# Flat maxima, norm scales later, a new order, and the weight groups' loads on Pool's queue

## The reference

```python
x = x + xattn(layernorm(x), ctx, ctx, q_norm_w, k_norm_w, w_out)
x = x + ffn(layernorm(x), ...)
# xattn: 16 query heads on 4 key heads, width 32; RMS norms with weights, rotary positions,
#        scores * 1/sqrt(32), causal mask, softmax, times v, then @ w_out.T
# ffn:   y1 = x1 @ w_up + b_up + x1 @ a_up @ b_up_lora ; x2 = relu(y1)
#        y2 = x2 @ w_down + b_down + x2 @ a_down @ b_down_lora
# w_up, w_down: 2048 x 512 and 512 x 2048, (q - 7.5) * scale, one scale for 64 columns, q stored as int32
```

## Time and profile before

| | us |
|---|---|
| median of 3 runs (lowest, highest) | 485.68 (484.91, 486.22) |
| profiled execution, its time | 485.92 |
| its span, first to last instruction | 484.1 |
| TensorE (PE) busy | 442.8 (91%) |
| VectorE (DVE) busy | 352.2 (73%) |
| ScalarE (ACT) busy | 300.2 (62%) |
| Pool busy | 282.2 (58%) |

### The profile page before, as it was taken

How to read it: one execution, slowest core, us unless ns; L and a number is a source line. 1 busy time by engine, 2 the same in 40 slices (tenths; PEclk the granted TensorE clock), 3 DMA queues, 4 the chain that set the end, 5 groups by cost and what they waited for, 6 DMA issues and landing times.

```text
span 484.1 us, 8263 instructions
## 1 busy us (share of the span) xinstructions
PE 442.8 (91%) x2416; PEld 217.4 (45%) x2416; DVE 352.2 (73%) x1078; ACT 300.2 (62%) x927; POOL 282.2 (58%) x304
## 2 busy tenths in 40 slices
PE   0266859999999999999999999999999999999997
PEld 0254535444444444444444444444444444444443
DVE  3999898979879786868686877778777856544341
ACT  1599788877848575758575766667575846522120
POOL 5367677776758584838484747565666745351100
PEclk9996699999999999999999999999999999999999
DMA  5686869779866877988777687887678677474422
GB/s 147 258 261 142 190 208 213 134 146 144 169 130 123 167 118 154 130 174 123 162 134 152 132 168 131 169 126 159 125 144 158 115 151 113 91 122 97 88 56 74
DMA packets 207372, 70.17 MB, mean 145 GB/s; under 512 B 196912, under 2 KB 199728, under 8 KB 206688
## 3 DMA queue, kind: packets, MB, share of 16 engines
q1 hardware_dynamic: 205760, 69.09, 71.6%
q10 hardware_dynamic: 1488, 0.40, 0.4%
q0 software_dynamic: 80, 0.16, 0.1%
HBM read 16.95 MB, written 4.19 MB: 44 GB/s over the span
## 4 chain that ended last, share of the span: by engine, by line
PE 78%; DVE 1%; DMA 1%; SPq 0%; issue 0%
PE ff L936 33%; PE ff L922 32%; PE tb L904 7%; PE sb L876 2%; PE tb L892 2%; DMA x<-hid 1%; SPq L393 0%; PE tb L862 0%; DVE t_sin L1147 0%; DVE pr L1179 0%; DVE y L1229 0%; DVE stats L1160 0%; DVE x L1157 0%; DVE q L1188 0%; DVE wd_lo L1081 0%; DVE q L1096 0%
## 5 line engine op out<-in xcount | busy, mean ns | idle before, releaser
L936 PE MATMUL ff<-wd_hi,x 128*128 128x512 f16 x512 | 152.3, 379 | 0.6 <-DMA x<-hid 0.6
L922 PE MATMUL ff<-wu_hi,xnT 128*128 128x512 f16 x512 | 152.5, 379 | 0.2 <-ACT wu_lo L641 0.2
L679 ACT ACTIVATE pr<-pr,nmax 128x128 f32<-128x128 f32 x256 | 99.1, 389 | 14.6 <-DVE nmax L1179 13.9
L505 POOL TENSOR_TENSOR big<-pr,big 128x512 f16<-128x512 f32 x64 | 80.9, 1271 | 33.6 <-ACT big L710 33.5
L922 PE MATMUL ff<-wu_lo,xnT 128*128 128x512 f16 x256 | 97.0, 379 | 0.0
L936 PE MATMUL ff<-wd_lo,x 128*128 128x512 f16 x256 | 97.0, 379 | 0.0
L496 POOL TENSOR_TENSOR pr<-pr,rinv 128x512 f32<-128x512 f32 x64 | 72.7, 1137 | 35.7 <-DVE rinv L1089 35.7
L744 ACT ACTIVATE hid<-z 128x512 f16<-128x512 f32 x64 | 39.9, 624 | 80.5 <-DVE z L1110 80.5
L1179 DVE CUSTOM_DVE_ANT_0 pr<-sb,tabs,score_scale 128x128 f32<-128x128 f32 x256 | 73.8, 344 | 12.3 <-PE sb L876 11.2
L922 PEld LDWEIGHTS ff<-wu_hi,xnT 128*128 128x128 f16 x512 | 48.0, 98 | 58.9 <-issue 5.9
L1110 DVE SCALAR_TENSOR_TENSOR z<-ff,su,b_row 128x512 f32<-128x512 f32 x64 | 47.6, 744 | 36.0 <-PE ff L922 34.7
(11 more groups left out here) (149 smaller groups left out, 652.2 us busy)
## 6 DMA issues: line engine op xcount, KB each, us to landing
xt<-in_x SPq DMA_DIRECT2D x16, 256.0 KB, 3.1
big<-in_L_ffn_w_up_q SPq DMA_DIRECT2D x4, 1024.0 KB, 5.6
big<-in_L_ffn_w_down_q SPq DMA_DIRECT2D x4, 1024.0 KB, 6.3
out<-y SPq DMA_DIRECT2D x16, 256.0 KB, 2.7
kvt<-in_ctx SPq DMA_DIRECT2D x16, 64.0 KB, 2.9
wd_lo<-in_L_xattn_w_out SPq DMA_DIRECT2D x1, 1024.0 KB, 7.9
pT<-big SPq DMA_TRANSPOSE x64, 3.5
b_row<-in_L_ffn_b_up SPq DMA_DIRECT2D x1, 1024.0 KB, 9.2
```

Source lines behind the costliest of these rows:

```text
L505: pool.tensor_tensor(p3[:, m, :, 1, :], pr[:, m], p3[:, m, :, 0, :], ALU.subtract).then_inc(p_low, 1)
L679: last = act.activation(pr[:, m, g, :], pr[:, m, g, :], ACT.Exp, bias=nmax[:, p, j:j + 1], scale=-1.0, accum_out=rsum[:, p, j:j + 1])
L922: last = pe.matmul(bank[:], a[:, m, :], b[:, m, 512 * g:512 * g + 512], start=(m == 0 and i == 0), stop=(m == KC - 1 and i == 2))
L936: last = pe.matmul(ff[down_bank[n]][:], x2T[:, part, k + h % HG, :], b[:, h, :], start=(h == 0 and i == 0), stop=(h == HC - 1 and i == 2))
```

## The change

The kernel after differs in these parts:

- The maxima of s_up, of the down lora matrix and of the bias are taken of flat copies with long contiguous pieces (in the third stage buffer); s_up and the down lora matrix are loaded again in their own layout, s_up in four parts. The rest of s_up is scaled later (`later_scales`, ahead of the first VectorE tile from 4 on). The identity part of the tables comes in a load of its own.
- `norm_scales` (with the norm powers in it) and the moments of batch 0 stand in the loop, at slots 19 and 20; only the two maxima of the norm weights stay ahead.
- 13 scale steps in place of 17; the lora halves wait for 10 of them and are done apart for up and down.
- All tables of the order are new. VectorE dequantizes 25 tiles in place of 27 (Pool: 10, 16, 19, 22, 23, 27, 30) and writes 28 low halves in place of 25.
- Group 0 is loaded on SP without its waits. Groups 1 to 7 are loaded from Pool's queue, inside Pool's loop, with the same waits, and group 2 also after the maxima.

```diff
-R_MOMENTS = (0, 23, 473, 1390)
+R_MOMENTS = (20, 77, 760, 1674)
...
-DVE_TILES = (0, 1, 2, 3, 4, 5, 6, 7, 8, 9, 10, 12, 13, 14, 15, 16, 17, 18, 19, 20, 22, 23, 24, 25, 27, 28, 30)
+DVE_TILES = (0, 1, 2, 3, 4, 5, 6, 7, 8, 9, 11, 12, 13, 14, 15, 17, 18, 20, 21, 24, 25, 26, 28, 29, 31)
...
-LOAD_AT = (369, 421, 557, 574, 1092, 1168, 1277)
+LOAD_AT = (182, 210, 281, 692, 890, 1237, 1432)
...
+LORA_D_LOAD_AT, NORM_SCALES_AT = 137, 19
...
+        s_up_flat, a_dn_flat = big[:, 4096:4096 + HC * C // QB], big[:, 4224:4224 + HC * R]
+        b_flat = big[0:HC, 4480:4480 + P]
...
-            def load_group(g):
-                if g >= W_RING:
-                    sp.wait_ge(w_turned, 4 * (g - W_RING + 1))
-                src = wuq_v[g] if g < 4 else wdq_v[g - 4]
-                sp.dma_start(stage_i[:, g % W_RING], src).then_inc(wq_in[g % W_RING], 16)
...
             sp.dma_start(s_dn[:], wds.rearrange("(p c) b -> p c b", p=P)).then_inc(scales_in, 16)
+            sp.dma_start(a_dn_flat, wda.rearrange("(p c) r -> p (c r)", p=P)).then_inc(lora_a_in, 16)
+            sp.dma_start(xt[:, 0, :], x[0]).then_inc(x_in[0], 16)
...
-            load_batch(0)
-            sp.wait_ge(lora_a_in, 16 * 3)
-            sp.wait_ge(k_weight_in, 16)
-            sp.wait_ge(q_weight_in, 16)
-            load_group(0)
+            sp.dma_start(s_up[:, 0:4, :].rearrange("p i b -> p (i b)"), wus_v[0]).then_inc(up_scales_in[0], 16)
+            sp.dma_start(stage_i[:, 0], wuq_v[0]).then_inc(w0_in, 16)
+            for g in range(1, 4):
+                sp.dma_start(s_up[:, 4 * g:4 * g + 4, :].rearrange("p i b -> p (i b)"), wus_v[g]).then_inc(up_scales_in[1], 16)
...
+            def load_group(g):
+                if g >= W_RING:
+                    pool.wait_ge(w_turned, 4 * (g - W_RING + 1))
+                if g == 2:
+                    pool.wait_ge(tops_ready, 7)
+                src = wuq_v[g] if g < 4 else wdq_v[g - 4]
+                pool.dma_start(stage_i[:, g % W_RING], src).then_inc(wq_in[g % W_RING], 16)
...
             for s in range(SLOTS):
+                for g in range(1, 8):
+                    if LOAD_AT[g - 1] == s:
+                        load_group(g)
...
+            def later_scales():
+                dve.wait_ge(up_scales_in[1], 16 * 3)
+                dve.tensor_scalar(s_up[:, 4:, :], s_up[:, 4:, :], kap[:, 0:1], None, ALU.mult).then_inc(scales_ready, 1)
+                dve.wait_ge(scales_ready, 3)
...
             find_tops()
-            norm_powers()
             gather_tops()
             input_stats(0)
-            norm_scales()
-            input_moments(0)
-            take_tops()
+            norm_tops()
             find_scales()
             for s in range(1, SLOTS):
+                if s == NORM_SCALES_AT:
+                    norm_scales()
```

More of the change, by code:

```diff
@@ new lines @@
+R_MOMENTS = (20, 77, 760, 1674)
+R_KEYS = (0, 284, 671, 2018)
+R_POW = (130, 280, 886, 2236)
+R_CENTRE = (18, 59, 913, 1980)
+R_SINES = (44, 152, 960, 1733)
+R_COSINES = (181, 209, 1210, 2240)
+R_ROPE = (108, 341, 980, 1738)
+R_KSPLIT = (45, 407, 1176, 2046)
+R_KLOW = (134, 345, 1081, 1794)
+R_KTURN = (247, 545, 854, 1798)
+R_QSPLIT = (94, 463, 1093, 2051)
+R_QLOW = (146, 410, 1067, 1763)
+R_QTURN = (212, 392, 829, 1794)
+R_SCORES = ((281, 643, 1348, 2033), (480, 674, 1397, 2052), (500, 876, 1551, 2129), (591, 1020, 1692, 2159))
@@ L242, in build @@
         tops_taken = sem("tops_taken")
+        up_scales_in, a_dn_in = [sem(f"up_scales_in{i}") for i in range(2)], sem("a_dn_in")
         scale_steps, scales_ready = sem("scale_steps"), sem("scales_ready")
@@ L754, in _ @@
                 second_norm_high(s)
-                if s == LORA_A_AT:
-                    lora_a_high()
+                for down in range(2):
+                    if LORA_A_AT[down] == s:
+                        lora_a_high(down)
                 if LORA_BHIGH_AT == s:
@@ L1016, in gather_tops, with find_scales @@
                 dve.tensor_scalar(diag8[:], ident[0:8, 0:8], top8[:], None, ALU.mult).then_inc(diag8_ready, 1)
-            def take_tops():
+            def find_scales():
+                bound, power, lora, deq = tmp[:, 0:5], tmp[:, 5:10], tmp[:, 10:12], tmp[:, 12:14]
                 dve.wait_ge(tops_spread, 1)
+                link(dve.tensor_scalar(deq, tb[0][:, 0:2], 7.5 / W_TOP, 1e-30 / W_TOP, ALU.mult, ALU.add), wait=False)
+                link(dve.tensor_scalar(lora, tb[0][:, 2:4], float(R) / W_TOP, None, ALU.mult), wait=False)
+                link(dve.tensor_scalar(bound[:, 2:4], tb[0][:, 2:4], 1e-30, 1.0 / A_TOP, ALU.add, ALU.mult), wait=False)
@@ new lines, in find_scales @@
+                dve.wait_ge(scale_steps, 3)
+                for j in range(2):
+                    link(dve.tensor_scalar(bound[:, j:j + 1], lora[:, j:j + 1], tops_all[:, 4 + j:5 + j], deq[:, j:j + 1], ALU.mult, ALU.add), wait=j > 0)
+                link(dve.tensor_scalar(bound[:, 4:5], bound[:, 0:1], float(C) * W_TOP, tops_all[:, 6:7], ALU.mult, ALU.add))
+                link(dve.tensor_scalar(power.bitcast(I32), bound.bitcast(I32), 0x7F800000, None, ALU.bitwise_and))
+                link(dve.reciprocal(kap[:, 0:5], power))
@@ new lines, in find_scales @@
+                for j in range(2):
+                    link(dve.tensor_scalar(kap[:, 6 + j:7 + j], kap[:, j:j + 1], power[:, 2 + j:3 + j], None, ALU.mult), wait=False)
+                assert step[0] == LORA_STEPS
+                dve.wait_ge(up_scales_in[0], 16)
+                dve.tensor_scalar(s_up[:, 0:4, :], s_up[:, 0:4, :], kap[:, 0:1], None, ALU.mult).then_inc(scales_ready, 1)
+                dve.tensor_scalar(s_dn[:], s_dn[:], kap[:, 1:2], None, ALU.mult).then_inc(scales_ready, 1)
+                link(dve.tensor_scalar(kap[:, 5:6], kap[:, 4:5], X2_TOP, None, ALU.mult))
@@ L1248, in _ @@
                     wout_arg()
-                if s == LORA_ALOW_AT:
-                    lora_a_low()
+                for down in range(2):
+                    if LORA_ALOW_AT[down] == s:
+                        lora_a_low(down)
                 if LORA_BLOW_AT == s:
```

252 lines of the change are left out of this document (117 added, 135 removed).

## The result

The changed kernel takes 495.38 us (median of 4 runs, 493.71 to 497.4), against 485.74 us for the kernel before beside it (484.91 to 486.22): ratio 1.020, 95% interval 1.017 to 1.023. It is slower, as forecast, but by 9.6 us and not by 4.1, and so above the range, which ended at 494.5.

A forecast was written before the change was run, and what follows sets the result against it. VectorE was taken to bound the front, setting when TensorE becomes full. Start 4.0 us earlier, list +6.4, waits +0.8 and Pool's chain put tile 20 5.0 later; minus 0.45 and 0.5 gave +4.1: 489.8 us, range 482.8 to 494.5.

The forecast's parts named there:

- The sign and where it is decided: Whole kernel: slower by 4.1 us, decided before TensorE becomes full at tile 20; the part from 110 us on unchanged.
- The start: Scales ahead of VectorE's loop: last maximum at 8.8 us, then 6.3 us, so the loop begins at 15.0, 4.0 us earlier.
- VectorE's list ahead of tile 19, +6.4 us: VectorE's added work before tile 17's low half frees tile 19's bank, including norm scales, moments and low halves: +6.4 us.
- I take 0.8 us of waits for both: VectorE's waits for the second and third weight groups, loaded from Pool: 0.8 us together, between 0 and 2.5.
- Pool's chain behind tile 19: After tile 19 is turned, Pool issues the last load, then does two dequantizations: 5.2 us before tile 20, starting 5.0 later.
- On SP the moved loads leave room: SP's queue: its 13.6 us of waits at the moved loads go, but a query transpose there was ready no sooner.
- so I count no gain: SP's queue, freed of the moved loads, was given no gain in the sum: 0 us.
- the wait of group 8: Pool's last load, called group 7 in the prediction, waits for tile 19's turn and holds up two dequantizations that tile 20 needs.
- The clock: TensorE at tile 20: a gap over 5 us may drop it to 1.2 GHz, giving 492 us; counted inside the forecast's range.
- The 0.95 us that I took off behind tile 20: TensorE behind tile 20: 0.45 us for two score groups done earlier and 0.5 us of shrinking waits, subtracted.
- Pool's loads are slow: Pool's seven loads cost 1.5 us each to issue or land 2 us late: 493 to 495 us, chance 0.1.

The follow-up runs named there:

- experiment 1: Changed kernel with weight groups 2 to 8 loaded from SP's queue again, order tables as changed: 485.26 us, ratio 0.999.
- experiment 10: Changed kernel, loads on Pool, with the last group's load moved behind the dequantizations of tiles 22 and 23: 491.46 us, ratio 1.013.
- experiment 12: Changed kernel, loads on Pool, with loads of groups 4, 6 and 8 moved behind other work and groups 5 and 7 moved off transpositions: 489.61 us, ratio 1.008.
- experiment 3: Kernel before with groups 2 to 8 loaded from Pool's queue, the first three of these loads placed early: 497.39 us, ratio 1.023.
- experiment 5: Kernel before, loads on SP, with group 8's load one slot earlier, ahead of batch 2's key transposition: 487.90 us, ratio 1.004.
- experiment 4: Kernel before, loads on Pool, first three early, groups 6 and 8 behind the transpositions, SP's three waits for turned tiles kept: 487.58 us, ratio 1.005.
- experiment 6: Kernel before, loads on SP, with group 5's load moved behind batch 1's query and key transpositions: 488.62 us, ratio 1.005.
- experiment 13: Changed kernel, loads on Pool, with the value sums of batch 0 behind tile 8 in TensorE's list: 495.81 us, ratio 1.019.
- experiment 14: Changed kernel with its loads on SP and the value sums of batch 0 behind tile 8 in TensorE's list: 485.36 us, ratio 0.999.
- experiment 7: Kernel before with the new maxima, norm scales and scale steps, old order, loads on SP, group 5's load behind batch 1's transpositions: 488.06 us, ratio 1.004.
- experiment 8: Changed kernel with its loads on SP and group 5's load moved behind batch 1's key transposition: 486.50 us, ratio 1.001.
- experiment 9: Changed kernel, loads on SP, group 5's load behind batch 1's key transposition, value sums of batch 0 behind tile 8: 485.54 us, ratio 1.000.
- experiment 2: Kernel before with only groups 2 to 8 loaded from Pool's queue, every other order as before: 498.25 us, ratio 1.027.

## Why the prediction was wrong

- **The sign and where it is decided: right.** From 120 to 480 us TensorE is busy for 360.0 of 360 us in both kernels; the loss is made ahead of that.
- **The start: too cautious.** The loop begins 5.4 us sooner, not 4.0: the last maximum ends 1.8 us ahead of the 8.8 that I took, and from it to the loop are 6.7 us, not 6.3. The norm scales cost 1.2 us in the loop, not 2.1: two integer instructions of half the size took 0.2 us together and not the 1.19 of the one in the earlier trace rows.
- **VectorE's list ahead of tile 19, +6.4 us: the number right, in part by luck.** With the loads on SP tile 19 is turned at 71.9 (experiment 1); the forecast said 71.7. But the loop begins at 14.1 there and the norm scales are 0.9 us cheaper, so about 1.8 us should have come on top and did not. VectorE, taken as always busy, is idle for 6.2 us from 20 to 100, and what TensorE waits for just ahead of tile 19 is batch 2's scores (1.4 us), not a low half.
- **"I take 0.8 us of waits for both" for groups 2 and 3: right** (0.7 us at VectorE).
- **Pool's chain behind tile 19: right.** From tile 19 turned to tile 20's transposes 4.9 us, forecast 5.2; taken away it gives 3.9 us back (experiment 10).
- **The step that failed is the one on what the moved loads leave behind: "On SP the moved loads leave room", and "so I count no gain".** It asked whether SP would gain and not whether anything would lose by the loads' new place, and it counted them on Pool as issue time and waits alone: its sum has no term for them between group 3 and group 8. The 3.9 us by which tile 19 is later than with the loads on SP are missing there. Between these two traces, which run the same list, the lag grows in three steps. First, Pool's load of group 5 leaves at 43.30, and batch 1's key transposition, at 44.20, lands in 6.3 us; with the loads on SP it lands in 2.5 us (the changed kernel, then experiment 1):

```profile
DMA to landing us min/median/max: 6.3/6.3/6.3
```

```profile
DMA to landing us min/median/max: 2.5/2.5/2.5
```

  The scores of batch 1 wait 3.4 us behind it. But they wait 2.6 us in experiment 1 as well, where group 5's load on SP delays the query transposition instead, and the lag at this place is 1.4 us. Second, Pool stands 4.2 us at the load of group 6, and its work behind that load then runs at the same time as three instructions of VectorE, which take 3.8 us together instead of 2.1. The longest of them, the changed kernel, then experiment 1:

```profile
59.19 1.75 DVE L1099 SCALAR_TENSOR_TENSOR big<-big,s_dn 128x512 f32<-128x512 int32 x1
```

```profile
57.47 0.69 DVE L1099 SCALAR_TENSOR_TENSOR big<-big,s_dn 128x512 f32<-128x512 int32 x1
```

  In experiment 12, where Pool's work lies elsewhere, each of the three takes 0.68 us. With that the first output projection starts 2.9 us late. Third, TensorE has by then waited 3.1 us for it and not 1.7, and does these matmuls at half clock and not at full, 5.1 us in place of 2.6 (windows, as before):

```profile
63.34:68.44 5.10, 5.10 (x13) 1.80 (x14) 3.03 (x5) 3.11 (x12) 3.90 (x4) 0.50 0.56 109
```

```profile
60.43:63.03 2.60, 2.60 (x12) 1.19 (x13) 2.09 (x5) 2.60 (x6) 0.46 (x1) 1.00 0.99 347
```

  That makes 5.4 us, of which experiment 1 gives back 1.5 up to tile 19 by a longer wait and half clock of its own. The three steps are read from one trace of each; no experiment takes them apart. Pool's load of group 7, at 63.80, holds batch 2's query transposition up too (7.3 us), but the scores ahead of tile 19 wait 1.6 us for it, against 1.4 in experiment 1, so it adds next to nothing here. I had priced the wait of group 8 alone; those of groups 4 and 6 are 5.0 and 4.2 us.
- **The clock: a rival that came true.** I had it inside the forecast. The gap of 4.5 us left TensorE at half clock from 80.7 to about 86, and the lag behind experiment 1, 8.1 us at tile 20, is 9.9 us at the end. The 0.95 us that I took off behind tile 20 do not show.
- **The rival "Pool's loads are slow": wrong by its own terms.** They took 0.57 to 0.82 us each to issue and 5.3 to 8.5 us to land, near SP's 4.8 to 9.6, and groups 2 and 3 cost next to nothing. But its time, 493 to 495, was the nearest to the truth, by luck: the loads were not slow, they made others slow. The Trainium skill (DMA: Bandwidth & Descriptors, section Issuing engines are not separate DMA queues) says that loads of all issuers end on the same 16 engines and interleave there. I used it to count no gain. The runs fit it: a load held a key transposition up from Pool's queue and from SP's own (10.0 and 6.4 us, experiments 3 and 5), and that is the side of it for which I had no term.

In sum, the queue costs 10.1 us. By the two traces 3.9 are lost ahead of tile 19 as above, 4.3 in Pool's chain behind it, and 1.8 at half clock behind that. By the experiments 3.9 come back with the last load moved, 1.8 with four others, and 4.3 were not taken apart, with 9.0 us of Pool's waits still in that kernel. The new order costs 1.5, and the front gives back 2. That loads hold transpositions up is shown in the kernel before by adding a collision (experiments 3 and 5) and by taking one away (4 and 6); that this made most of its 12 us rests on experiment 4, which moved more than that. In the changed kernel the direct share of it is small in the trace, 1.4 us at batch 1's scores.

## What to carry to other kernels

In-order queues carry an order between transfers that nothing in the code states: before a load is moved to another queue, list the small latency-bound transfers on the old one and see which of them the load will now start beside. Price a moved wait at every instance and for all that is queued behind it, and the queue that it leaves as well, since that wait may have been holding back something else. And the largest wait of an engine is not yet a cost: moving it gave nothing (experiments 13 and 14), while one slot of one load gave or took 2 to 4 us (experiments 5, 6, 7 and 10). A load taken off one transposition falls on the next (experiments 6 to 9 and 12), so look at all that will run under it at its new place.

## What was not expected of the hardware

- A key transposition that lands in 2.4 to 3.4 us takes 6.3 to 10.0 us when a 1 MB load was issued 0.9 to 1.1 us ahead of it, from Pool's queue or from SP's own (experiments 2, 3 and 5 and the changed kernel); with two such loads leaving 0.5 and 1.6 us behind it, a probability block took 7.3 us (experiment 3) in place of 3.3.
- Its issue is held up too: the query transposition behind group 5's load takes SP 3.5 us before and 5.4 us in experiment 1, in place of 1.7 to 1.9, and so all that follows on SP is late.
- The same integer instruction of VectorE on 128x2 elements took 1.19 us before and 0.47 us in experiment 3.
- The same wait of TensorE, 2.88 us ahead of tile 20, left the clock at full in the profiled execution of the kernel before and at half in those of experiments 3 and 5. Two traces can differ by 2 to 3 us for this alone.
- VectorE's dequantization of a 128x512 tile took 0.69 us while Pool was idle and 1.75 us while Pool worked on tiles of the same size (experiment 1 and the changed kernel); Pool's cosine product took 1.72 us there and 1.27 in experiment 1.
